# A fused attention and mixture-of-experts kernel: the first batch's transposes moved in front of the last shared step, and their split in front of the shared result's addition

## The reference, cut to what matters

```python
x = x + L0_xattn(layernorm(x), ctx)          # attention probabilities
x = x + L0_ffn(layernorm(x))                 # top-2 of 8 experts with capacity, plus
                                             # 0.2 * (gelu(xt@sw1+sb1)@sw2+sb2 + gelu(xt@swd)@swu)
x = x + L1_xattn(ctx, ctx, mask, layernorm(x))   # scores * layernorm(x), masked, softmax
x = x + L1_ffn(layernorm(x))                 # (silu(x@Wg.T) * (x@Wu.T)) @ Wd.T, W = lut[idx]
```

## Time and profile before

| | |
|---|---|
| Time, median of 3 runs | 324.44 us (321.94 to 325.86) |
| The profiled execution's own time | 326.25 us |
| Its span, first to last instruction | 324.5 us |
| TensorE matmul busy | 302.0 us, 93% |
| TensorE weight loads busy | 258.8 us, 80% |
| VectorE busy | 240.4 us, 74% |
| ScalarE busy | 153.9 us, 47% |
| GpSimd busy | 110.9 us, 34% |
| Mean granted TensorE clock | 0.968 of full |

### The profile page before, as it was taken

One profiled execution on the slowest core, in us unless ns is written; L12 is line 12 of the kernel. 1 busy time (PEld: TensorE's weight loads), 2 busy tenths in 40 slices (PEclk: granted clock), 3 DMA queues, 4 the chain that ended last, 5 costly groups with the idle time before them and its releaser, 6 DMA issues.

```text
span 324.5 us, 5969 instructions
## 1 busy us (share of the span) xinstructions
PE 302.0 (93%) x1920; PEld 258.8 (80%) x1920; DVE 240.4 (74%) x650; ACT 153.9 (47%) x360; POOL 110.9 (34%) x153
## 2 busy tenths in 40 slices
PE   8998677997899999999999999999999979989895
PEld 4654455775789989898998989899888869979795
DVE  4658987411488989899898989899885848796742
ACT  3466437442345556454655555464641732634210
POOL 8483643672000503205060411406051205442432
PEclk9997759999799999999999999999999999999999
DMA  7994018324348493937557391936225000010101
GB/s 223 374 273 107 10 40 266 125 83 127 103 130 252 97 313 66 288 105 209 160 129 267 69 329 58 249 119 151 85 26 144 4 0 2 0 33 2 34 1 65
DMA packets 26259, 41.51 MB, mean 128 GB/s; under 512 B 3898, under 2 KB 16955, under 8 KB 26236
## 3 DMA queue, kind: packets, MB, share of 16 engines
q1 hardware_dynamic: 22012, 36.49, 35.4%
q0 software_dynamic: 4224, 4.75, 8.2%
HBM read 31.40 MB, written 9.82 MB: 127 GB/s over the span
## 4 chain that ended last, share of the span: by engine, by line
PE 69%; DVE 14%; DMA 5%; issue 4%; POOL 4%; ACT 2%; another core or an unknown queue 1%; SPq 1%; POOLq 0%; DVEq 0%; ACTq 0%
PE hb L718 23%; PE yb L737 20%; PE hb L855 7%; PE yb L751 5%; PE tb L651 3%; PE rb L870 3%; PE yb L870 3%; PE yb L855 2%; DVE bst L1115 2%; POOL xbuf_dram L501 2%; DVE xn L1121 1%; DVE x L1260 1%; DMA x<-x_dram 1%; DMA xacc_dram<-ysb,slot_i 1%
## 5 line engine op out<-in xcount | busy, mean ns | idle before, releaser
L737 PE MATMUL yb<-raw,h 128*128 128x256 f32 x384 | 96.6, 381 | 0.5 <-ACT h L1021 0.5
L1021 ACT ACTIVATE h<-hb,b 128x320 f32<-128x320 f32 (+1 forms) x80 | 44.6, 559 | 69.9 <-PE hb L718 61.7
L737 PEld LDWEIGHTS yb<-raw,h 128*128 128x128 f32 x384 | 70.2, 191 | 8.0 <-ACT h L1021 0.9
L718 PE MATMUL hb<-xT_hi,w_hi 128*128 128x320 f32 (+1 forms) x180 | 72.5, 403 | 1.5 <-DVE xT_lo L1273 1.5
L521 POOL DMA_INDIRECT xacc_dram<-ysb,slot_i x16 | 25.1, 1568 | 125.9 <-ACT ysb L889 123.5
L718 PE MATMUL hb<-xT_lo,w_hi 128*128 128x320 f32 (+1 forms) x180 | 59.5, 331 | 0.0
L718 PE MATMUL hb<-xT_hi,w_lo 128*128 128x320 f32 (+1 forms) x180 | 59.3, 330 | 0.0
L1465 DVE TENSOR_TENSOR w_lo<-raw,w_hi 128x256 fp32r<-128x256 f32 x81 | 33.7, 416 | 18.9 <-ACT w_hi L889 13.4
L1147 DVE COPY_PREDICATED pick<-bits,pick 128x544 int32<-128x544 uint8 x56 | 43.2, 771 | 0.6
L718 PEld LDWEIGHTS hb<-xT_hi,w_hi 128*128 128x128 f32 x180 | 34.4, 191 | 6.7 <-issue 2.0
L718 PEld LDWEIGHTS hb<-xT_hi,w_lo 128*128 128x128 f32 x180 | 34.5, 192 | 2.5
(11 more groups left out here) (216 smaller groups left out, 534.9 us busy)
## 6 DMA issues: line engine op xcount, KB each, us to landing
raw<-w1pack_dram SPq DMA_DIRECT2D x30, 384.0 KB, 3.5
raw<-w2pack_dram SPq DMA_DIRECT2D x30, 384.0 KB, 5.1
xbuf_dram<-h SPq DMA_DIRECT2D x8, 323.8 KB, 9.3
idx<-idx_dram SPq DMA_DIRECT2D x8, 272.0 KB, 6.0
xg<-xbuf_dram SPq DMA_DIRECT2D x8, 259.0 KB, 5.9
x<-x_dram SPq DMA_DIRECT2D x4, 256.0 KB, 4.0
xacc_dram<-x SPq DMA_DIRECT2D x2, 512.0 KB
x<-xacc_dram SPq DMA_DIRECT2D x4, 256.0 KB, 5.0
```

The costliest lines, as they stand in the source:

```text
L718: mm = pe.matmul(hb[s % RING][:, 0:n], w[:, s, k * P:(k + 1) * P], a[:, turn, k, 0:n], start=(i == 0), stop=(i == len(terms) - 1))
L737: mm = pe.matmul(yb[c // 2][:, (c % 2) * D:(c % 2 + 1) * D], h, w, start=(s == 0 and c % 2 == 0), stop=(s == STEPS - 1), skip_group_check= ...
L1021: act.activation(hidden(s - 1, shared, turn), bank[:, 0:n], ACT.Gelu, bias=b1[:, expert, s - 1:s])\
```

## The change

TensorE: the last two `second` steps of unit 9 are no longer issued together. Step 7 is issued, then the four transposes of batch 0, then step 8, and then the wait for the looked-up weights. VectorE: `x3T_split(0)` is issued ahead of the two waits for x_back and of `add_shared(1)`. ScalarE, GpSimd and SyncE are as they were. No instruction is added or removed.

```diff
@@ TensorE
             unit(E + 1, 1, shared=True)
-            for s in range(STEPS - LAG, STEPS):
-                second(E + 1, s, True, 1)
...
+            for s in range(STEPS - LAG, STEPS - 1):
+                second(E + 1, s, True, 1)
+            transpose_x3(0)
+            second(E + 1, STEPS - 1, True, 1)
             pe.wait_ge(lk, JOBS * JOPS)
-            transpose_x3(0)
             for n in range(B * NG + GLAG):
@@ VectorE
+            x3T_split(0)
             for later in range(2, B):
                 dve.wait_ge(x_back[later], 16)
             add_shared(1)
-            x3T_split(0)
             for n in range(B * NG):
```

## The result

The changed kernel takes 322.29 us in the median of 22 runs (319.84 to 327.47) and the kernel before 323.94 in 22 runs (321.94 to 325.86). The ratio is 0.9942, 95% interval 0.992 to 0.9964: 0.6% faster, which is 1.9 us of 323.94. It leaves out the changed kernel's five longest runs (324.90 us and more), which count as slow for lying over 1.5% above its fastest, and no run of the kernel before. With every run counted the medians differ by 1.65 us and the means by 0.87 (322.90 against 323.77), so 1.9 is the upper of three readings. Its size is better read from the trace.

A forecast was written before the change was run, and what follows sets the result against it. TensorE bounds the kernel, pausing at the seam for batch 0's split behind VectorE's addition. Closing the whole 1.94 us pause, rounded to 1.9, takes the median from 324.44 to 322.5 us; range 320.0 to 325.1.

The forecast's parts named there:

- The pause is the wait for the split: TensorE before the last layer's first gate matmul: 1.74 us without matmuls until batch 0's low split is done; 1.94 us to gain.
- The rival of an instruction fetch: TensorE's pause before the first gate matmul is fetching of instructions, so nothing is won: 324.4 us; chance 8%.
- Transposes between steps 7 and 8, with xn ahead by 0.84: TensorE, shared expert's end: VectorE's normalised batch 0 (xn) ready 0.84 us before the transposes' turn; they delay step 8 by 0.57.
- The seam, 3.95 us: Stretch from step 7's start on TensorE to the last layer's first gate matmul: 3.95 us, before 5.89.
- My 1.66: TensorE's time in us to issue one of the shared expert's last two steps, from 16 weight loads in 3.32 us.
- The addition's cover of 0.34: VectorE: the shared result's addition ends at 266.03, 0.34 us before the products of n = 0 are called for.
- The price of an addition 1 us later still: Rival on VectorE: an addition ending d us later loses d - 0.34; a d of 1 gives 323.1 us; no separate chance.
- The gain carried whole to the end: Last layer: later waits move along with its start, so 1.94 us reaches the end; 58.3 us from first gate matmul.
- The tail: Stretch from the last layer's first gate matmul to the span's end; forecast 58.3 us, as before.
- Late xn: Rival: xn at 263.65 or later holds transposes and step 8, gain 0.25 us, 324.2; with other partial gains 9%.
- My formula, 2.30 us: From the transposes' start through copy and split to the first gate matmul: 2.30 us after the change, 2.55 before.
- The clock: Rival: moved pauses in the last layer lower TensorE's clock for 8 us, 4 us lost: 326.5 us or more; 3%.

The follow-up runs named there:

- TensorE's half alone: Changed kernel with VectorE's old order, the addition of the shared result ahead of x3T_split(0); ratio 1.0035 to the kernel before.
- The added VectorE work: Changed kernel plus two VectorE subtractions with unused results, behind add_shared(1) and ahead of the products of n = 0; ratio 0.995 to the kernel before.
- GpSimd was kept away: Kernel with the two extra VectorE subtractions, where GpSimd's low part of n = 4 also waits for VectorE's batch 2 offsets; ratio 0.9943 to the kernel before.
- the one kernel where xn was late at this place: Changed kernel with ScalarE's batch 1 exponentials behind the last Gelu and VectorE's add_probs for batch 1's first tile behind x3T_split(0); ratio 0.9915 to the kernel before.

## Why the prediction was right

The forecast was 322.5 us and a gain of 1.9. The median is 322.29, the medians differ by 1.65 and the ratio gives 1.9. That the time came out so near is in part luck: 322.5 was counted from 324.44, the median of three runs, and the 22 runs of the kernel before have 323.94, from which the same gain leads to 322.0. What the trace bears out is the gain in the seam. Point by point:

**The pause is the wait for the split, and the chance order of three engines makes it.** Shown from both sides: with only one half of the change the matmuls pause 2.18 or 1.50 us, with both not at all. The rival of an instruction fetch falls with that, since the pause followed the split in every kernel, by 0.14 or 0.15 us after its end.

**Transposes between steps 7 and 8, with xn ahead by 0.84.** It was 0.80. Their price to step 8 was put at 0.57; from 263.56 to the next load at 264.11 it was 0.55, and TensorE's half alone lost 0.57.

**The seam, 3.95 us.** 3.94 in both executions of the changed kernel. One refinement: where TensorE has not waited for Gelu ahead of step 7 it is 4.06 or 4.07, because the step then takes 1.72 and not 1.59 us. My 1.66 was the mean of one of each.

**The addition's cover of 0.34.** It was 0.45: the addition began at 266.25, 4.31 us behind step 7's first load, where I had worked out 264.74 - 260.30 = 4.44. The price of an addition 1 us later still was a little too low in the forecast: 322.5 + 0.66 = 323.2, not 323.1; no run had that case at the seam. The error in the cover was on the safe side: step 8's results stood at 264.21 + 1.89 = 266.10, 4.16 us behind step 7's first load, and not 264.61 - 260.30 = 4.31; the row of that last step's matmuls is not shown above.

**The gain carried whole to the end.** The tail is 58.3 before and after. My ground for it was that every later wait moves along with the start. The added VectorE work showed that the tail has room besides: a first product 0.67 us late cost nothing at the end once GpSimd was kept away. I had thought VectorE's queue tight from n = 0 on; up to batch 1's split it is not.

**Late xn.** Put on trial by moving the transposes once more: held in order, 0.7 us lost, and still much less than the pause of before. The rival's own case, xn so late that only 0.25 us is gained, no run tried. My formula, 2.30 us from the start of the transposes to the gate matmul, measured 263.45 - 261.29 = 2.16 in the one kernel where xn was late at this place.

**The clock** was granted in full, 1.00, from 256 to 272 and to the end of the span in every window read. By the rule cited in the prediction from the Trainium skill ("TensorE: Matmul & The Clock Gate", "Part 1: The HAM clock gate"), that activity raises the clock, the denser seam should not have cost it, and the trace agrees.

The doubt in the forecast was in the times, not the sum: the changed kernel's runs spread over 7.6 us, four times the gain.

## What to carry to other kernels

Where a chain goes through several in-order queues, an early input is worth nothing until the instruction stands early in its own queue too: of this change one half alone was a loss and the other next to nothing, and together they closed the pause. The place for the early work is the latest one at which it still hides, here one step of 1.7 us before the end; one step further and it held up what it was to pass. And when the seam is closed, list the waits of the bound engine over the whole stage behind it: four waits of 0.5 to 1.1 us, all behind VectorE work that was queued after a Silu whose result it did not need and that then ran into GpSimd, were worth more than the seam.

## What was not expected of the hardware

GpSimd can hold a VectorE operation for the time of its own. Two operations of the same form took 0.95 and 0.49 us; the first ran beside GpSimd's L537 (269.57 to 271.00) and ended at 271.27, 0.27 behind it. With GpSimd kept away both took under 0.49. The changed kernel has the same in its last layer:

```profile
282.85 1.42 POOL L537 TENSOR_TENSOR h_lo<-h,h_hi 128x256 fp32r<-128x256 f32 x2 [1.01 <-DVE h L1535]
...
283.54 1.02 DVE L1260 SCALAR_TENSOR_TENSOR x<-xg,rsum,x 128x256 f32<-128x256 f32 x1
...
285.15 0.45 DVE L1260 SCALAR_TENSOR_TENSOR x<-xg,rsum,x 128x256 f32<-128x256 f32 x1
```

The first L1260 ends 0.29 us behind GpSimd, the second has VectorE's side to itself and takes 0.45. Both take two operands from SBUF. The Trainium skill has this in "SBUF — State Buffer", section "Who interferes with whom": a VectorE instruction with two SBUF inputs contends with a GpSimd instruction that reads SBUF, the ports that they share are an exclusive lock, and the order of issue decides which of the two is blocked. The trace agrees that VectorE's operation is held until GpSimd's is done; it then needed only 0.27 to 0.29 us more, not its full 0.45 to 0.49. The other direction fits too, though no run put it to trial: in the changed kernel GpSimd's L537 that starts at 268.81, while VectorE's L1260 runs (268.65 to 269.13), takes 0.91 us, where a single one elsewhere in this layer takes 0.72 to 0.74.
